# Low softmax weights against V's high part alone, one product behind each transpose of the odd steps, in a two-layer attention kernel

## What is computed

```python
xn  = group_norm(x, 32 groups) * norm_w + norm_b
qkv = W_qkv @ xn + b_qkv              # 8 heads of D = 64 channels
w   = softmax(scale * q.T @ k)        # 1024 x 1024 for each head
a   = w @ v
out = x + W_proj @ a + b_proj
```

## Time and profile before

| | us |
|---|---|
| median of 3 runs | 4347.31 (4347.17 to 4347.99) |
| span of the profiled execution | 4346.0 |
| PE busy | 4295.6 (99%) |
| weight loads busy | 3736.9 (86%) |
| DVE busy | 3313.6 (76%) |
| ACT busy | 2875.3 (66%) |
| POOL busy | 2505.1 (58%) |

### The profile page before, as it was taken

One profiled execution on the slowest core, in us unless ns is written; L12 is line 12 of the kernel. 1 busy time (PEld: TensorE's weight loads), 2 busy tenths in 40 slices (PEclk: granted clock), 3 DMA queues, 4 the chain that ended last, 5 costly groups with the idle time before them and its releaser, 6 DMA issues.

```text
span 4346.0 us, 89905 instructions
## 1 busy us (share of the span) xinstructions
PE 4295.6 (99%) x26692; PEld 3736.9 (86%) x26692; DVE 3313.6 (76%) x5483; ACT 2875.3 (66%) x5317; POOL 2505.1 (58%) x2406
## 2 busy tenths in 40 slices
PE   7999999999999999999999999999999999999999
PEld 6888888888888888888888888888888888888887
DVE  5777867788687786777867778687786877868778
ACT  4757747477474775747757476574765747667476
POOL 5655556565564655656566565565655646556465
PEclk9999999999999999999999999999999999999999
DMA  3232222322223222222222222222222222223222
GB/s 87 48 96 47 71 72 48 96 47 80 64 46 96 49 78 64 56 86 49 80 71 66 81 46 80 65 66 79 48 79 64 71 71 49 79 64 82 60 49 92
DMA packets 99933, 295.61 MB, mean 68 GB/s; under 512 B 15136, under 2 KB 15264, under 8 KB 99616
## 3 DMA queue, kind: packets, MB, share of 16 engines
q1 hardware_dynamic: 99616, 291.71, 25.0%
HBM read 123.88 MB, written 33.55 MB: 36 GB/s over the span
## 4 chain that ended last, share of the span: by engine, by line
PE 95%; DVE 2%; issue 1%; POOL 1%; ACT 1%; DMA 0%; SPq 0%; DVEq 0%; ACTq 0%; POOLq 0%
PE ps_t L760 21%; PE ps_g L714 15%; PE ps_o L772 11%; PE ps_o L773 11%; PE ps_s L751 11%; PE ps_s L749 11%; PE ps_s L714 7%; PE ps_t L714 6%; PE ps_o L714 3%; POOL x_raw L389 1%; ACT probs L479 0%; DVE spread L603 0%; DVE pt_lo L569 0%; DVE work L601 0%; PE ps_t L778 0%
## 5 line engine op out<-in xcount | busy, mean ns | idle before, releaser
L383 POOL TENSOR_SCALAR probs<-probs,row_rcp 128x1024 f32<-128x1024 f32 x1024 | 1149.9, 1123 | 1375.5 <-DVE row_rcp L564 1374.0
L560 DVE TENSOR_REDUCE row_min<-ps_s 128x1 f32<-128x1024 f32 x1024 | 1250.2, 1221 | 220.5 <-PE ps_s L751 205.0
L484 ACT CAST pt_hi<-ps_t 128x512 fp32r<-128x512 f32 x2048 | 1110.6, 590 | 446.5 <-PE ps_t L760 431.7
L569 DVE TENSOR_TENSOR pt_lo<-ps_t,pt_hi 128x512 fp32r<-128x512 f32 x2048 | 1308.5, 679 | 9.5 <-ACT pt_hi L484 5.0
L479 ACT ACTIVATE probs<-ps_s,row_min 128x1024 f32<-128x1024 f32 x1024 | 1150.7, 1124 | 215.5 <-DVE row_min L560 202.5
L760 PEld LDWEIGHTS ps_t<-const_sb,probs 128*128 128x128 f32 x8192 | 944.3, 140 | 185.5 <-DVE pt_lo L569 57.0
L760 PE MATMUL ps_t<-const_sb,probs 128*128 128x128 f32 x8192 | 1085.9, 274 | 0.8
L772 PE MATMUL ps_o<-pt_hi,v_st 128*128 128x256 f32 x4096 | 1044.4, 288 | 0.0
L773 PE MATMUL ps_o<-pt_lo,v_st 128*128 128x256 f32 x4096 | 1014.8, 282 | 0.0
L751 PE MATMUL ps_s<-kl_st,q_st 128*128 128x512 f32 x2048 | 808.3, 395 | 0.0
L772 PEld LDWEIGHTS ps_o<-pt_hi,v_st 128*128 128x128 f32 x4096 | 771.6, 188 | 39.4 <-issue 12.4
(11 more groups left out here) (110 smaller groups left out, 4918.2 us busy)
## 6 DMA issues: line engine op xcount, KB each, us to landing
wqk_raw<-in_wqk SPq DMA_DIRECT2D x130, 256.0 KB, 2.7
q_st<-kh_st SPq DMA_DIRECT2D x128, 256.0 KB, 2.9
q_st<-kl_st SPq DMA_DIRECT2D x128, 256.0 KB, 3.6
kh_st<-kh_st SPq DMA_DIRECT2D x128, 256.0 KB, 2.9
kl_st<-kl_st SPq DMA_DIRECT2D x128, 256.0 KB, 3.5
x_raw<-layer_out SPq DMA_DIRECT2D x36, 512.0 KB, 5.0
wv_raw<-in_wv SPq DMA_DIRECT2D x68, 256.0 KB, 3.6
x_raw<-in_x SPq DMA_DIRECT2D x32, 512.0 KB, 5.3
```

Source lines behind the costliest of these rows:

```text
L383: nc.gpsimd.tensor_scalar(probs[m % 2][:, :], probs[m % 2][:, :], row_rcp[:, m % 4:m % 4 + 1], 1.0, ALU.mult, ALU.mult).then_inc(probs_rea ...
L484: nc.scalar.copy(pt_hi[:, m // 2 % 2, 4 * half:4 * half + 4, (m % 2) * P:(m % 2 + 1) * P], ps_t[:, half, :].rearrange("p (b t) -> p b t", ...
L560: nc.vector.tensor_reduce(row_min[:, m % 4:m % 4 + 1], ps_s[:, m % 2, :], AX.X, ALU.min).then_inc(min_ready, 1)
L569: nc.vector.tensor_tensor(pt_lo[place], ps_t[:, half, :].rearrange("p (b t) -> p b t", b=4), f32(pt_hi[place]), ALU.subtract).then_inc(lo_ ...
```

## The change

The low softmax weights are multiplied with V's high part alone (`weigh_low`: 64 stationary columns, into partitions 0 to 63 of `ps_o`); the product of the two low parts is left out. The eight low products of a group move from between the high products of two steps to the odd step, one behind each of its transposes. The high products 0 to 6 of a group stand in the even step, and the eighth, which closes the group, behind the projections of the odd step. Group 7 keeps its place and takes its eight low products in a row. V leaves PSUM by a plain copy, and its bias is added where the two halves of `ps_o` are added, as a per-partition scalar.

```diff
-                nc.vector.tensor_tensor(attn[rows, cols], ps_o[rows, 0:GROUP], o_part[k % 2][rows, :],
-                                        ALU.add).then_inc(attn_ready, 1)
+                nc.vector.scalar_tensor_tensor(out=attn[rows, cols], in0=ps_o[rows, 0:GROUP],
+                                               scalar=bv_sb[rows, bass.ds(lay * KT + p, 1)], in1=o_part[k % 2][rows, :],
+                                               op0=ALU.add, op1=ALU.add).then_inc(attn_ready, 1)
...
-                nc.vector.tensor_tensor(v_raw[:, b, :].rearrange("p (o n) -> p o n", o=1),
-                                        v_bank[b].rearrange("p (o n) -> p o n", o=1),
-                                        bv_all[:, bass.ds(lay, 1), :], ALU.add).then_inc(v_evac, 1)
+                nc.vector.tensor_copy(v_raw[:, b, :], v_bank[b]).then_inc(v_evac, 1)
...
+            def weigh_high(k, b):
+
+                mm = nc.tensor.matmul(ps_o[:, 0:GROUP], v_st[k // 4][:, b, :], pt_hi[:, k % 2, b, :],
+                                      start=(b == 0), stop=(b == BLK - 1))
+                if b == BLK - 1:
+                    mm.then_inc(pv_done, 1)
+
+            def weigh_low(k, b):
+
+                nc.tensor.matmul(ps_o[0:D, 0:GROUP], v_st[k // 4][:, b, 0:D], pt_lo[:, k % 2, b, :],
+                                 start=False, stop=False)
...
+            def transpose_and_weigh(n, m, k):
+
                 pe.wait_ge(probs_ready, n + 1)
+                for c in range(BLK):
+                    if c % 4 == 0:
+                        pe.wait_ge(lo_ready, lo_at(n - 1, c // 4))
+                    transpose(m, c)
+                    if k is not None and m % 2 == 1:
+                        weigh_low(k, c)
+
+            def last_group(tile, g, hd):
+                group_free(tile, g, hd, 7)
+                weigh_high(7, 0)
+                for b in range(BLK):
+                    weigh_low(7, b)
+                for b in range(1, BLK):
+                    weigh_high(7, b)
...
-                        if m >= 2:
-                            k = (m - 2) // 2
-                            weigh(tile, 8 * pair + k, H * i + 2 * p + k // 4, k, 4 * (m % 2), 4 * (m % 2) + 4)
+                        if k is not None and m % 2 == 0:
+                            group_free(tile, 8 * pair + k, H * i + 2 * p + k // 4, k)
+                            for b in range(BLK - 1):
+                                weigh_high(k, b)
+                        elif k is not None:
+                            weigh_high(k, BLK - 1)
```

More of the change, by code:

```diff
@@ L119, in build @@
         bo_sb = sb("bo_sb", [P, LAYERS * KT], F32)
+        bv_sb = sb("bv_sb", [P, LAYERS * KT], F32)
         nw_sb = sb("nw_sb", [P, LAYERS * KT], F32)
@@ L280, in _ @@
             sp.dma_start(nb_sb[:, :], nb).then_inc(const_loaded, 16)
[L281 removed]
+            sp.dma_start(bv_sb[:, :], bv).then_inc(const_loaded, 16)
             load_wqk(0, 0)
@@ L570, in low_part, with add_halves @@
                                         f32(pt_hi[place]), ALU.subtract).then_inc(lo_ready, 1)
-            def add_halves(pair, k):
+            def add_halves(pair, lay, p, k):
                 rows = slice(0, D) if k < 4 else slice(D, P)
@@ L627, in x_low, with evac_v @@
                                         ALU.subtract).then_inc(xn_ready, 1)
-            def evac_v(i, lay, b):
+            def evac_v(i, b):
                 dve.wait_ge(v_acc, 8 * i + b + 1)
-                nc.vector.tensor_tensor(v_raw[:, b, :].rearrange("p (o n) -> p o n", o=1),
-                                        v_bank[b].rearrange("p (o n) -> p o n", o=1),
-                                        bv_all[:, bass.ds(lay, 1), :], ALU.add).then_inc(v_evac, 1)
+                nc.vector.tensor_copy(v_raw[:, b, :], v_bank[b]).then_inc(v_evac, 1)
             def output(i, lay, q):
@@ L662, in _, with pair_steps @@
                 x_low(0, c)
-            def pair_steps(i, p, last):
+            def pair_steps(i, lay, p, last):
                 pair = PAIRS * i + p
@@ L668, in pair_steps @@
                     if not last and m >= 4 and m % 2 == 0:
-                        add_halves(pair, m // 2 - 2)
+                        add_halves(pair, lay, p, m // 2 - 2)
                     if not (last and m + 2 >= PT_STEPS):
@@ L674, in pair_steps @@
                     if m == PT_STEPS - 1 or last and m >= 3 and m % 2 == 1:
-                        add_halves(pair, (m - 3) // 2)
+                        add_halves(pair, lay, p, (m - 3) // 2)
                     if not (last and m + 2 >= PT_STEPS):
@@ L685, in pair_steps @@
                     group_spread(i + 1)
-                add_halves(pair, 7)
+                add_halves(pair, lay, p, 7)
             with dve.Fori(0, PASSES) as i:
@@ L690, in _ @@
                 for b in range(4):
-                    evac_v(i, lay, b)
+                    evac_v(i, b)
                 for m in range(2):
                     smallest(TILES * i + m, m)
-                    evac_v(i, lay, 4 + 2 * m)
+                    evac_v(i, 4 + 2 * m)
                     reciprocal(TILES * i + m, m)
-                    evac_v(i, lay, 5 + 2 * m)
+                    evac_v(i, 5 + 2 * m)
                 with dve.Fori(0, PAIRS - 1) as p:
-                    pair_steps(i, p, False)
-                pair_steps(i, PAIRS - 1, True)
+                    pair_steps(i, lay, p, False)
+                pair_steps(i, lay, PAIRS - 1, True)
                 norm_coefs(i + 1, within(next_pass(i) // B, 0, LAYERS - 1))
@@ L753, in scores @@
                 mm.then_inc(scores_ready, 1)
-            def transpose(n, m):
-                pe.wait_ge(probs_ready, n + 1)
[L757 to L775, removed]
+            def transpose(m, c):
+                mm = nc.tensor.transpose(ps_t[:, c // 4, (c % 4) * P:(c % 4 + 1) * P],
+                                         probs[m % 2][:, c * P:(c + 1) * P], ident)
+                if c % 4 == 3:
+                    mm.then_inc(transposed, 1)
@@ new lines, in weigh_high, with group_free @@
+            def weigh_high(k, b):
[6 more added lines that the diff above has]
+                                 start=False, stop=False)
+            def group_free(tile, g, hd, k):
+                pe.wait_ge(attn_ready, sum_at(g - 1))
+                pe.wait_ge(v_ready, hd + 1)
+                pe.wait_ge(lo_ready, lo_at(tile + 2 * k + 1, 1))
@@ L821, in pair_steps @@
                             project(0, 3, 6)
-                        transpose(tile + m, m)
+                        k = (m - 2) // 2 if m >= 2 else None
+                        transpose_and_weigh(tile + m, m, k)
                         if not last and m < PT_STEPS - 1:
@@ L872, in _ @@
                     pair = PAIRS * i + p
-                    weigh(TILES * i + PT_STEPS * p, 8 * pair + 7, H * i + 2 * p + 1, 7, 0, BLK)
+                    last_group(TILES * i + PT_STEPS * p, 8 * pair + 7, H * i + 2 * p + 1)
                 pair_steps(i, PAIRS - 1, True)
@@ L921 @@
         "bqk": columns(qkv_b[:, :, 0:2].reshape(LAYERS, H * P)),
-        "bv": qkv_b[:, :, 2].reshape(LAYERS, C),
+        "bv": columns(qkv_b[:, :, 2].reshape(LAYERS, C)),
         "bo": columns(both("proj_b", "out_b")),
```

3 lines of the change are left out of this document (1 added, 2 removed).

## The result

The changed kernel takes **4493.51 us** (median of 4 runs, 4492.82 to 4494.83); the kernel before took 4347.65 beside it (4 runs, 4347.17 to 4349.13). The ratio is 1.0335, 95% interval 1.032 to 1.0349: 146 us slower. Forecast were 4460, 113 slower, with 4285 to 4500 as the range.

The account below looks back on a forecast made before the run. PE, busy 99% of the span, was taken to set the pace. New waits of 91 us in pairs 0 to 2 plus 23 in the last pair, 114 on 4346, gave 4460 us; range 4285 to 4500, the case's own 4400 to 4500.

Parts of the forecast that it names:

- A transpose with its low product costs 0.23: On PE in odd steps: transpose 0.11 plus low product 0.119 us, as before apart; the load doesn't space them.
- Rival B: Faster: a product behind a transpose starts once its half-sized load is in, 0.06; 4307 us, chance 0.26.
- Rival D: Far slower: the array drains between the two shapes, 0.16 at 7168 places; 5500 us, chance 0.02.
- The late eighth transpose delays ACT and then DVE, and PE waits: Odd steps: eighth transpose 0.83 us later, delaying high_part to add_halves, for which PE's next group waits; 0.36 to spare.
- Rival C: No change: ACT and DVE reorder their slack so that PE hardly waits; 4347 us, chance 0.08.
- Behind step 3: Pairs 0 to 2: addition chain done at 5.53, PE ready at 5.15, so PE waits 0.38 us.
- Behind 7 and 11: Pairs 0 to 2: the same wait for the addition, 0.38 us behind step 7 and 0.61 behind step 11.
- step 15: Pairs 0 to 2: group 7 starts 0.64 us later, 0.12 of it the ninth product, so 0.52 more.
- The last pair: ACT reaches other_half 2.43 instead of 2.19 behind the transposes: 0.24 more, 6 times a pass, 16 passes, 23 us.
- The three-operand addition: add_halves with V's bias as third operand: 0.03 us longer, half of 743 against 691 ns at 512 columns.
- The copy in `evac_v` at nothing: V's copy instead of an addition, 128 instructions of 691 ns: no effect, as PE's pace hides them.
- The change of kind at +0.005 or -0.009 a product: Bounds on PE: 64-column low products -32 us (3584 x 0.009), change of kind +36 us (7168 places); middle taken.

Follow-up runs that it names:

- e3_lows_wide: The changed kernel with low products of 128 stationary columns instead of 64 (V's low part included again): 4506.76 us, ratio 1.0368 to the kernel before.
- e10_behind_add_two: The changed kernel with the eight low products together behind the eight transposes and V's bias added in evac_v as before: 4355.06 us, ratio 1.0014.
- e5_add_two: The changed kernel with V's bias added in evac_v as before and a two-operand addition of the halves: 4457.28 us, ratio 1.0252.

## Why the prediction was right, and where its terms were off

The direction, the mechanism and the place were right; the size was 33 us short.

1. **A transpose with its low product costs 0.23.** Right: 1520.49, 1520.72, 1520.95, and e3_lows_wide shows that doubling the load moves the spacing by 3 ns. Rival B falls with that. By the Trainium skill (TensorE: Matmul & The Clock Gate, "LDWEIGHTS (loading the stationary operand)"), whose load time goes by the columns alone, the transposes would be spaced by their loads and the pair would take an estimated 0.05 less; these rows don't agree. Rival D falls too: a product of 64 columns behind a full transpose drained nothing, the pair costs 0.23 where D had over 0.3 from one matmul to the next.

2. **The late eighth transpose delays ACT and then DVE, and PE waits.** Right, and shown by where the eighth transpose stands: with the same products on PE the time is 4372 with it at 0.77, 4386 at 1.24, 4493 at 1.59 and 4527 at 1.69. The number of changes of kind doesn't order them: in an odd step it is 1, 9, 15 and 2. Rival C falls: the queues gave nothing back but the slack.

3. **Behind step 3**: forecast a product start of 5.53 against PE ready at 5.15, a wait of 0.38. Measured 5.69 against 5.13 (step 4's start at 3.56, and 1.57 from there as in e10_behind_add_two), 0.56. Without the bias's part it is 0.25 (e5_add_two), less than the 0.35 of the sum, chiefly since from the end of the addition to the product that waits for it pass 0.15 there and not the 0.24 read ahead of group 7 in the earlier trace rows. Behind 7 and 11 in the same way 0.24 and 0.50 where 0.35 and 0.58 were forecast without the bias; step 15 came as forecast: 0.62 longer with its ninth product, where the sum has 0.61 without the bias. In all, pairs 0 to 2 got 1.56 x 48 = 75 us longer instead of 85 (1.77 without the bias): the three waits were 0.29 shorter than forecast, and 0.12 came in steps 13 and 14, which the sum left free (6.53 together against 6.41 before); the rest is the exchange of products.

4. **The last pair**: forecast 0.24 x 6 x 16 = 23 us, measured 2.06 x 16 = 33 (e5_add_two). The term that is off is the 0.48 from the start of the second `high_part` to `other_half`: that was the distance to an exponential, which starts before the `high_part` ahead of it is over. `other_half` starts when it is over. The changed kernel's timeline of ACT, last pair, step 9 (its first transpose is stamped 1654.23 with 0.33 instead of the usual 0.27, since it waited, so it starts at 1654.29, as the 1589.98 of the forecast was stamped 1589.92):

```profile
1656.20 0.59 ACT L464 CAST pt_hi<-ps_t 128x512 fp32r<-128x512 f32 x1 [0.33 <-PE ps_t L736]
...
1656.82 0.37 ACT L471 COPY o_part<-ps_o 64x256 f32<-64x256 f32 x1
```

0.62 instead of 0.48, so with the second `high_part` at 1.91 instead of 1.95 the copy starts 2.53 behind the first transpose instead of 2.43, and 0.10 x 6 x 16 = 10 us more, all that was missing.

5. **The three-operand addition**: forecast 0.03 at each waiting place, 6 us in all; measured 36. This is the step that failed, 30 of the 33 us. The sum took half of 52 ns, as if the cost went with the elements, where the measured addition is 61 longer at 256 columns, and counted it at four places of a pair where six got longer (19 us); and the column index worked out at run time, a part of the diff to which the sum gave nothing, delays the first and fifth addition of a pair (17 us).

6. **The copy in `evac_v` at nothing**: right, and it isn't even shorter (691 ns as before).

7. **The change of kind at +0.005 or -0.009 a product**: the measured gain of a 64-column product is 3 ns, inside the bounds, 11 us.

The sum by experiments: from the kernel before 7 us for the uneven split with its small products (e10_behind_add_two), 102 for the interleaving (e5_add_two), 36 for the bias (the changed kernel). That the order's share comes out as forecast, 109 against 108, is partly luck: 10 too much in pairs 0 to 2 and 10 too little in the last.

## What to carry to other kernels

Work put between instructions whose result another engine awaits costs no more on its own engine than elsewhere (0.23 for a transpose and its product here), and yet moves the last of them by all that stands between; compare that with the slack of the chain behind it, and put the work behind the last one instead. An operand chosen at run time had its address worked out on the queue of the engine that uses it, behind the wait (17 us here): copy it to a fixed place where the engine idles. And a saving in one place (V's bias out of an addition that PE's pace hid) is no reason to lengthen an operation on the path.

## What the runs showed of the hardware that was not expected

- DVE's addition of 64x256 elements takes 421 ns with two operands and 483 with a third per-partition operand; but a copy of 128x512 out of PSUM takes the same 691 as an addition with a second tile.
- The run-time column delayed an addition that was waiting by 0.25 us at the first group of a pair, and by 0.12 at the fifth, the first that reads the other 64 partitions; the additions between, which read the same columns, were not delayed.
- A 256-column product behind a transpose is recorded as starting 0.03 behind it and lasting 0.36, where the real spacing, by the next transpose and the product's own 0.12, is 0.11; mean durations (352 ns against 288) must not be read as slower products.
- A product that starts from a wait is recorded 0.10 early, with a duration longer by as much (seven last 1.10 instead of 1.00).
- Low products with 64 instead of 128 stationary columns gain 3 ns each (11 us for 3584 of them), though the load was hidden: twice the load behind a transpose costs no more than that.
